# Written-out chunk loops in a graph network's steps

## The reference

```
h = relu(layernorm(x))
5 times:
    messages = h[col] @ W_msg.T + b_msg
    agg = segment_sum(messages, row)
    gi, gh = agg @ W_ih.T + b_ih, h @ W_hh.T + b_hh      # three parts each: r, z, n
    r, z = sigmoid(i_r + h_r), sigmoid(i_z + h_z)
    n = tanh(i_n + r * h_n)
    h = (1 - z) * n + z * h
out = x + h
```

## Time and profile before

| | us |
|---|---|
| median of 2 runs | 6251.72 (6239.28 to 6264.16) |
| the profiled execution | 6248.37 |
| its span | 6246.6 |
| setup stage in it | 0 to 1104 |
| the five steps in it | 1104 to 6247 |

### The profile page before, as it was taken

The page is one execution under the profiler, slowest core; times in us unless marked ns, Lnnn a source line. Parts: engine busy times, 40 slices in busy tenths (PEclk is TensorE's granted clock), DMA queues, the critical chain, the costliest instruction groups (busy, mean ns, idle before and its releaser), DMA issues.

```text
span 6246.6 us, 261732 instructions
## 1 busy us (share of the span) xinstructions
PE 4820.9 (77%) x112184; PEld 3776.4 (60%) x112185; DVE 3473.5 (56%) x6216; ACT 3188.3 (51%) x6141; POOL 236.3 (4%) x254
## 2 busy tenths in 40 slices
PE   3664777788888877778888888888788887777777
PEld 1423665666666666666666666666666666666665
DVE  6998777455555554545555555555555554444444
ACT  6202777555555554545455555555555554444444
POOL 0000000000000000000000000000000000000000
PEclk8987888999999999999999999999999999999998
DMA  2002443333333332323323233333233333333332
GB/s 71 2 1 74 163 164 159 113 99 96 101 95 104 102 93 91 102 93 97 97 92 103 92 104 97 100 102 100 95 104 95 100 103 98 97 97 97 97 97 75
DMA packets 227296, 603.16 MB, mean 97 GB/s; under 512 B 23316, under 2 KB 143425, under 8 KB 225966
## 3 DMA queue, kind: packets, MB, share of 16 engines
q1 hardware_dynamic: 217950, 566.55, 27.4%
q0 software_dynamic: 8272, 19.43, 1.3%
HBM read 467.05 MB, written 118.84 MB: 94 GB/s over the span
## 4 chain that ended last, share of the span: by engine, by line
PE 65%; issue 16%; DVE 15%; ACT 2%; DMA 1%; DVEq 1%; SPq 0%; ACTq 0%; POOL 0%
PE f_ps_c L783 21%; PE f_ps_b L769 12%; PE f_ps_a L769 11%; PE f_ps_d L729 3%; PE f_ps_d L816 3%; PE f_ps_d L810 2%; PE f_ps_d L811 2%; PE f_ps_d L812 2%; DVE f_ring L979 2%; PE f_ps_c L803 2%; PE f_ps_d L817 2%; PE f_ps_d L818 2%; PE f_ps_c L823 2%; DVE f_ring L1118 2%; DVE f_hr L1123 1%
## 5 line engine op out<-in xcount | busy, mean ns | idle before, releaser
L783 PE MATMUL f_ps_c<-f_ring 128*32 128x256 f16 x49000 | 2595.7, 281 | 242.5 <-issue 200.5
L588 ACT CAST f_ring<-f_ps_b 128x512 f16<-128x512 f32 x2082 | 1185.0, 588 | 1299.8 <-PE f_ps_b L769 1293.8
L588 ACT CAST f_ring<-f_ps_a 128x512 f16<-128x512 f32 x2083 | 1191.2, 588 | 1157.8 <-PE f_ps_a L769 1151.6
L783 PEld LDWEIGHTS f_ps_c<-f_ring 128*32 128x32 fp8e4 x49000 | 1365.1, 99 | 473.5 <-issue 386.6
L769 PE MATMUL f_ps_b<-f_hr,f_ring 128*32 128x256 f16 x24496 | 1334.9, 281 | 286.1 <-issue 285.0
L769 PE MATMUL f_ps_a<-f_hr,f_ring 128*32 128x256 f16 x24504 | 1297.8, 282 | 200.0 <-issue 190.2
L1151 DVE CAST f_ring<-f_ps_b 128x512 f16<-128x512 f32 x980 | 673.4, 687 | 1085.0 <-PE f_ps_b L769 1084.3
L1151 DVE CAST f_ring<-f_ps_a 128x512 f16<-128x512 f32 x980 | 673.4, 687 | 932.3 <-PE f_ps_a L769 931.8
L769 PEld LDWEIGHTS f_ps_b<-f_hr,f_ring 128*32 128x32 fp8e4 x24496 | 682.7, 99 | 459.8 <-issue 441.0
L769 PEld LDWEIGHTS f_ps_a<-f_hr,f_ring 128*32 128x32 fp8e4 x24504 | 676.6, 99 | 358.8 <-issue 339.3
L508 POOL DMA_INDIRECT f_ring<-fast_hrows,f_idx_tab x245 | 231.1, 943 | 5927.0 <-PE f_ps_c L793 4588.3
(11 more groups left out here) (257 smaller groups left out, 5431.1 us busy)
## 6 DMA issues: line engine op xcount, KB each, us to landing
f_ring<-fast_adj_e SPq DMA_DIRECT2D x245, 800.0 KB, 4.6
f_ring<-fast_adj_o SPq DMA_DIRECT2D x245, 800.0 KB, 6.2
fast_adj_o<-f_ring SPq DMA_DIRECT2D x49, 800.0 KB, 3.4
fast_adj_e<-f_ring SPq DMA_DIRECT2D x49, 800.0 KB, 3.4
f_ring<-fast_deg SPq DMA_DIRECT2D x245, 128.0 KB, 6.2
fast_hrows<-f_hr SPq DMA_DIRECT2D x196, 128.0 KB, 1.8
fast_hrows<-f_hr SPq DMA_DIRECT2D x1, 6272.0 KB, 24.6
f_ring<-in_x_dram SPq DMA_DIRECT2D x48, 128.0 KB, 6.3
```

The costliest lines, as they stand in the source:

```text
L588: nc.scalar.copy(Gx[b], X[b]).then_inc(evac_a, 1)
L783: pe.matmul(R[ph % 2][32 * j:32 * j + 32, u * CW:(u + 1) * CW], lhsT=o[:, k * P + 32 * j:k * P + 32 * j + 32], rhs=kept[:, u * CW:(u + 1) ...
```

## The change

`run_step` becomes a loop of the program that writes the list: all 49 chunk bodies of a step stand one behind the other, on TensorE, VectorE and ScalarE. The number of a chunk is then a constant, and so is every value that is waited for and every place in `hT` and `hr`. The three counts of `pe_turns` on TensorE are dropped, so a wait stands on the matmul behind it.

```diff
-        def run_step(eng, s, body):
-            body(s, 0, 0)
-            with eng.Fori(0, (NCH - 1) // 4) as i:
-                for base in range(1, 5):
-                    body(s, base, i)
+        def run_step(s, body):
+            for c in range(NCH):
+                body(s, c, 0)
...
                 for s in range(STEPS):
-                    run_step(act, s, body)
+                    run_step(s, body)
...
                     if g == 0:
                         pe.wait_ge(hr_ready, n + 1)
-                    pe.sem_inc(pe_turns, 1)
                     kept = Gx[(ph + g) % RING]
...
                     pe.wait_ge(gathered[b], nh * 16 + 16)
                     pe.wait_ge(hs_ready, n + 1)
-                    pe.sem_inc(pe_turns, 1)
                     for u in range(2):
...
                             pe.wait_ge(e_loaded[ph % 2], nh * 16 + 16)
-                            pe.sem_inc(pe_turns, 1)
                         if base == 0 and s > 0:
...
                 for s in range(STEPS):
-                    run_step(pe, s, body)
+                    run_step(s, body)
...
                 for s in range(STEPS):
-                    run_step(dve, s, body)
+                    run_step(s, body)
```

## The result

The median went from 6251.72 us to **5251.79 us** (2 runs, 5249.61 to 5253.97): a ratio of 0.840, 95% interval 0.833 to 0.847. The forecast was 5858 us, with a range down to 5740. The direction is right and the size is not: 1000 us went, where 390 were forecast.

What follows compares the result with a forecast made beforehand. TensorE was taken to set the pace of the steps, with idle time from instruction delivery at jumps and packet stops. 6248.4 - 325 (jumps) - 65 (fewer packets) - 0 = 5858 us, range 5740 to 6030.

Steps and rivals of the forecast that it cites:

- Term 2: TensorE's list in the steps: 5.9% fewer instructions mean fewer packets and packet stops; 65 us saved, between 0 and 141.
- Term 1: TensorE's loop in the steps: the 55 jumps back go, saving 325 us, with a lower bound of 209 us.
- Term 3: VectorE and ScalarE: their wait registers and loops go, worth 0; at most 28.6 us touched if the cover fails.
- Term 4: SyncE's and GpSimd's unchanged lists: a chunk of about 19.3 us still leaves room for the next loads; 0 us.
- late next: TensorE's wait for the new h, 160.9 us before: time saved between the gates and that wait would lengthen it.
- the signs: Gathers all near 19.3 us, "issue" from 742 to about 500 us, 90 to 130 fewer packets, stops of 1 to 2 us remaining.
- Half of it stays: At TensorE's jumps, a packet stop replaces the idle time and the slow clock remains: 6078 us, chance 0.12.
- the jump is cheap: Idle time at the loop's head belongs to something else, such as the adjacency tile's wait: 6236 us, chance 0.04.
- A first reading costs more: TensorE's straight code is read once, each packet dearer than a repeated one: 6673 us at 1 us a packet, chance 0.03.
- More: Instruction delivery paces half of the steps: 5782 us or less; chance 0.06 for below 5780.

Runs made afterwards that it cites:

- the last experiment: Changed kernel with TensorE's turn of the new h at g = 23 and VectorE's new rows behind its cast of g = 22; median 5060.47 us.

## Why the prediction was wrong

The four corners, from runs above:

| | events that wait for the cast | no events |
|---|---|---|
| 55 long jumps | 6251.7 (before: jumps back, registers) | 5584.7 (forward jumps, constants) |
| no jump | 6254.4, 6236.2 (constants) | 5251.8 (after) |

- **Term 2 is the step that failed**, with its sentence that the register and event instructions are worth nothing in a flowing stretch. It gave 65 us, at most 141. With the jumps standing, dropping the events with their registers is worth 6251.7 - 5584.7 = 667 us, if a forward jump over 38 KB costs what the jump back does; without jumps the events are worth 1002. I saw that the stops lie 256 instructions apart in the middle of groups and took them for a property of the packets. The packets are as large in after, 814 of them are fetched in its steps, and TensorE's "issue" rows there sum to 38.0 us. A stop needs a packet that comes late as well, and with the events it does: the lowest quarter of the transfers begins 0.76 us ahead with the events and 2.96 us without. The steps of before had no stretch without events to show that; a flowing group's 0.22 us only said that an event takes no time of the array's own while the list is ahead.

- The size of a packet came out right by a wrong division: the 16.74 MB are TensorE's queue alone, the 261732 instructions those of all engines. In after 14.42 MB over TensorE's 225,181 instructions are 64 bytes; in before the packets that were fetched again made up for the other engines' instructions.

- The rule set aside in that step, that crossing a packet's boundary is mostly hidden (the Trainium skill, Runtime: NRT & Kernel Launch, Instruction fetch mechanics), holds in the list without these events, by the 38.0 us, and not in the one with them, by 680 us in the written-out list with events.

- **Term 1**, 325 us for 55 jumps, has the right size and the right picture (two stops, then the lower clock) for a list that flows: 5584.7 - 5251.8 = 333 us. That the two numbers lie so close is in part luck. Read over the first 46 gathers of each step, the excess in before is 25.8 - 19.4 = 6.4 us, or 352 us. And it was read as a gain that stands by itself. In the list with events and registers, 40 or 50 jumps fewer gained some 180 us, 4.5 or 3.7 us a jump, since the other chunks got longer; without any jump, and with constants for the registers, nothing that can be told was left (6236 to 6254 us). The terms don't add in either order.

- **Term 3** holds: 18 us at most from the loops of ScalarE and VectorE, by one run. **Term 4** holds: the gathers and loads kept up with a chunk of 16.56 us.

- What I had named as late next, the wait for h, did grow, by 71 us, which is small beside what went. But it also stood in the way of 191 us more, as the last experiment shows. The list of waits had it, with 232.1 us; VectorE's 36% of the chain is not the sign of it, since that share is still 35% when the wait is gone.

- Of the signs: no long fourth chunk, as said; packets of the steps fell by 142, a little more than the 90 to 130; "issue" fell to 38 and not to 500 us, and no stops of 1 to 2 us remained in number.

- The rivals. "Half of it stays" and "the jump is cheap" fell with after's even chunks and with the long jumps' 6.05 us. "A first reading costs more" fell too: after reads all its packets for the first time and barely stops. "More" had the right side and the wrong reason; delivery did cost TensorE most of its idle time, but not for the number of its instructions.

## What to carry to other kernels

When an engine stops for "issue" at a fixed spacing in its instructions, look at what holds its list before blaming the delivery. Here a wait on the matmul itself let the list run on, a wait on an instruction of its own ahead of it stopped the list, and that was worth 1000 us; even event instructions without a wait cost 347. An excess that is read off one place (a long fourth chunk) is a gain only if the places it is compared with stay as they are. Let a count that nobody waits for go, and after a large gain read the waits again: the next one was worth another 191 us for two moved lines.

## What the runs showed of the hardware that was not expected

- Event instructions ahead of TensorE's matmuls, 6,125 of them for a cast that had often not ended, cost 1002 us, 0.16 us each, although their own wait never shows in the list of waits; the same wait one group earlier cost 88 us over 6,124, 0.014 us each. 6,125 without any wait, behind the matmuls, cost 347 us, 0.06 us each.
- A packet of 256 instructions takes 1.0 us, and the first matmul behind it never started sooner than 1.13 us after it had landed (839 and 814 packets of two runs). Whether that shows is decided by when the transfer begins: 3.84 us ahead (median) in after.
- A taken jump of TensorE over 38 KB of instructions cost 6.05 us, of which some 2 x 3 us are stops, one packet each, followed by some 4 us at the lower clock; over 1 KB it cost 0.09 us, which can't be told from nothing.
- In the list with events and registers, with 55, 15 and 5 jumps, the chunks without a jump took 19.4, 19.8 and 20.1 us; in the two with constants and no jump 20.8 and 20.9. Why is open.
